# A graph network kernel on one core: first edge stage in another order, five source groups gathered later, another start, finer scatter turns

## The reference, cut to what matters

```python
# x: 100000 x 128, src and dst: 25000 edges, dst sorted (100000 * u**2)
def L0(x):      # edge messages, maximum by destination
    x_col = x[dst]
    feat = concatenate([x_col, x[src] - x_col], axis=-1)
    m = relu(feat @ W1 + b1) @ W2 + b2
    out = segment_max(m, dst, num_segments=x.shape[0])
    return where(isneginf(out), 0, out)
def L1(x):      # sum of neighbours, two-layer MLP, linear residual
    h = x + segment_sum(x[src], dst, num_segments=x.shape[0])
    h = maximum(h @ W1 + b1, 0) @ W2 + b2
    return x @ Wres + bres + h
x = layernorm(x + L0(x))
x = layernorm(x + L1(x))
```

## Time and profile before

| | us |
|---|---|
| median of 3 runs | 1114.47 |
| lowest and highest | 1114.39 and 1115.25 |
| the profiled execution, its own time | 1113.68 |
| its span (first to last instruction) | 1111.9 |
| PE busy in the span | 1068.9 (96%) |
| DVE busy | 934.9 (84%) |
| ACT busy | 896.9 (81%) |
| POOL busy | 765.8 (69%) |

### The profile page before, as it was taken

The page is one execution under the profiler, slowest core; times in us unless marked ns, Lnnn a source line. Parts: engine busy times, 40 slices in busy tenths (PEclk is TensorE's granted clock), DMA queues, the critical chain, the costliest instruction groups (busy, mean ns, idle before and its releaser), DMA issues.

```text
span 1111.9 us, 27074 instructions
## 1 busy us (share of the span) xinstructions
PE 1068.9 (96%) x7463; PEld 835.6 (75%) x7463; DVE 934.9 (84%) x3645; ACT 896.9 (81%) x3888; POOL 765.8 (69%) x798
## 2 busy tenths in 40 slices
PE   5899999999999999999899999999999999999995
PEld 3677877777666666666578888888888878888884
DVE  7799888897888888888868787878787789999993
ACT  2887878787888888888897888888888887777774
POOL 6777777777777777772047777777777777777712
PEclk9999999999999999999999999999999999999998
DMA  5788877875888888877576667676756566666652
GB/s 151 214 244 247 230 244 231 246 233 152 220 222 232 248 232 221 233 223 214 164 232 198 213 191 215 190 214 191 214 166 194 172 202 217 218 217 220 218 171 86
DMA packets 172255, 231.86 MB, mean 209 GB/s; under 512 B 25658, under 2 KB 90791, under 8 KB 172106
## 3 DMA queue, kind: packets, MB, share of 16 engines
q1 hardware_dynamic: 145434, 180.66, 52.0%
q0 software_dynamic: 25088, 48.94, 17.3%
q10 hardware_dynamic: 1584, 0.53, 0.2%
HBM read 129.48 MB, written 102.78 MB: 209 GB/s over the span
## 4 chain that ended last, share of the span: by engine, by line
PE 65%; POOL 19%; issue 8%; DVE 4%; ACT 2%; DMA 1%; SPq 0%; POOLq 0%; DVEq 0%; ACTq 0%
POOL edge_rows L522 17%; PE psY L1125 10%; PE psY L1126 10%; PE psH L1137 10%; PE psE L1118 6%; PE psT L1118 5%; PE psE L1257 4%; PE psE L1126 4%; PE psE L1125 4%; PE psE L1293 4%; PE psE L1248 3%; PE psE L1242 3%; PE psE L1240 3%; POOL xd_early L522 1%; DVE shared L758 1%
## 5 line engine op out<-in xcount | busy, mean ns | idle before, releaser
L1125 PE MATMUL psY<-wc,hT 128*128 128x128 f32 x1568 | 304.1, 276 | 0.5 <-DVE o_rows L646 0.4
L1126 PE MATMUL psY<-wcr,xT 128*128 128x128 f32 x1568 | 303.9, 276 | 0.0
L522 POOL DMA_INDIRECT edge_rows<-x1e_table,idx x196 | 188.8, 963 | 118.5 <-issue 59.4
L526 POOL DMA_INDIRECT out<-edge_rows,idx x196 | 195.0, 995 | 100.0 <-issue 61.9
L1125 PEld LDWEIGHTS psY<-wc,hT 128*128 128x128 f32 x1568 | 240.7, 192 | 13.3 <-issue 13.3
L949 ACT ACTIVATE junk<-psY 128x128 f32<-128x128 f32 x784 | 209.3, 302 | 49.3 <-PE psY L1126 49.1
L1126 PEld LDWEIGHTS psY<-wcr,xT 128*128 128x128 f32 x1568 | 238.8, 193 | 0.0
L522 POOL DMA_INDIRECT edge_rows<-in_x,idx x196 | 189.8, 968 | 65.5 <-issue 59.4
L609 DVE TENSOR_SCALAR x<-x_in,mv,rs 128x128 f32<-128x128 f32 x784 | 221.7, 361 | 0.6
L1137 PE MATMUL psH<-xT,wc 128*128 128x512 f32 x392 | 204.5, 604 | 6.2 <-ACT xT L944 5.5
L1118 PEld LDWEIGHTS psT<-ident,x 128*128 128x128 f32 x784 | 99.2, 143 | 110.1 <-issue 104.1
(11 more groups left out here) (125 smaller groups left out, 1993.4 us busy)
## 6 DMA issues: line engine op xcount, KB each, us to landing
x_in<-in_x SPq DMA_DIRECT2D x196, 256.0 KB
out<-o_rows SPq DMA_DIRECT2D x195, 256.0 KB
src_bc<-src_dram SPq DMA_DIRECT2D x49, 256.0 KB, 4.5
mask<-mask_dram SPq DMA_DIRECT2D x98, 128.0 KB
x1eT_spill<-x1eT SPq DMA_DIRECT2D x49, 256.0 KB, 2.4
x1e_table<-edge_rows SPq DMA_DIRECT2D x49, 256.0 KB, 3.5
x1e_table<-shared SPq DMA_DIRECT2D x49, 256.0 KB, 3.8
x1eT<-x1eT_spill SPq DMA_DIRECT2D x49, 256.0 KB, 3.1
```

The costliest lines, as they stand in the source:

```text
L522: nc.gpsimd.indirect_dma_start(to, None, table, bass.IndirectOffsetOnAxis(idx[:, what, t:t + 1], 0)).then_inc(landed[n % FLIGHT], 16)
L526: nc.gpsimd.indirect_dma_start(table, bass.IndirectOffsetOnAxis(idx[:, SCAT, t:t + 1], 0), frm, None, bounds_check=limit, oob_is_err=False ...
L1125: t_.matmul(to[:, cut(t)], h[:, cut(t)], wc2[:, :], start=t == 0, stop=False, skip_group_check=True)
L1126: last = t_.matmul(to[:, cut(t)], xt[:, cut(t)], wcr[:, :], start=False, stop=t == TILES - 1, skip_group_check=True)
```

## The change

Seven things change in the order and placing of work; no matrix product is added or removed.

1. In the first edge stage PE does `transpose_in(s+1)`, then `center_z(s-1)`, then `transpose_x1e(s-2)`, the reverse of before; `transpose_x1e` waits for one more `copy_xd`. DVE begins a step with the scan and the residual, and does the source statistics after `copy_xs`. ACT begins with `relu0`, and `copy_x1eT` comes behind the roots. The dense pieces of ACT and PE in `h` 0 and 1 change places.
2. The last five source groups (44 to 48) are gathered behind destination groups 12, 18, 24, 30 and 36, and no longer ahead of destination group 4.
3. SP loads unit 0 ahead of the source indices, and DVE takes its statistics first.
4. ACT issues the five bias loads after its first root, under a semaphore of their own. The copies of the combined weights go from DVE to ACT, and two of the weight products go behind the first dense product.
5. In the head ACT copies `xT` ahead of the root.
6. The first two `src_bc` loads are issued two steps' worth of queue entries earlier, at head step 6.
7. For groups 44 to 48, POOL waits for each slot's own count, worked out on DVE (`late_stores`, eight small instructions ahead of the second edge stage) and read with four register loads a turn.

```diff
-    SRC_FIRST = GROUPS
+    SRC_FIRST = GROUPS - 5
+    LATE_DST, LATE_EVERY = 12, 6
...
     def head(n):       # SP
...
+                if n == HEAD - 2:
+                    sp.wait_ge(s_srcst, 32)
+                    feed_s(0)
+                    feed_s(1)
...
+            load(0)
             sp.wait_ge(s_iz, 1)
             load_indices(0, src, s_is)
-            load(0)
             load(1)
...
             for g in range(SLOTS, GROUPS):
                 gather_dst(g)
+                if late_src_behind(g) is not None:
+                    gather_src(late_src_behind(g))
...
+            for g in range(LATE, WHOLE):
+                counts = late_needed(g - LATE)
+                pool.wait_ge(res_done, g + 1)
+                await_stores(counts)
+                for t in range(TILES):
+                    scatter_tile(g, t)
             for g in range(WHOLE, GROUPS):
                 pool.wait_ge(res_done, g + 1)
                 for t in range(TILES):
-                    await_stores(count if t < WHOLE_TILES else 16 * BODIES)
...
+                    await_stores(late_needed(SLOTS + t) if t < WHOLE_TILES else [16 * BODIES] * SLOTS)
+                    scatter_tile(g, t)
...
             def step_a(s, n, h):      # DVE
+                segment_max(s - 1)
+                residual0(s - 1)
                 both_recip(s)
                 scale_z(s)
-                segment_max(s - 1)
-                residual0(s - 1)
+                copy_xs(s + 1)
                 xs_stats(s)
                 xs_var(s)
-                copy_xs(s + 1)
...
             def head(n):       # ACT
-                if n == 0:
-                    copy_xT(0)
-                    root(0)
-                else:
-                    dense(n)
+                norm2_var(n - 3)
+                relu(n - 1)
+                copy_xT(n)
+                if n == 0:
+                    keep_weights()
+                root(n)
+                finish(n - 3)
...
             def step_a(s, n, h):      # ACT
+                relu0(s)
                 scale_xs(s)
-                relu0(s)
-                copy_x1eT(s - 2)
+                copy_xd(s + 1)
                 z_var(s - 1)
                 both_roots(s + 1)
-                copy_xd(s + 1)
+                copy_x1eT(s - 2)
...
             root(-2)
+            load_biases()
             root(-1)
-            act.wait_ge(s_w, 16 * 11)
+            act.wait_ge(s_b, 16 * 5)
...
             def step_a(s, n, h):      # PE
...
+                transpose_in(s + 1)
+                center_z(s - 1)
                 transpose_x1e(s - 2)
-                center_z(s - 1)
-                transpose_in(s + 1)
```

More of the change, by code:

```diff
@@ L159, in gnn_program @@
         s_w = sem("weights_loaded")
+        s_b = sem("biases_loaded")
         s_i = sem("indices_loaded")
@@ L254, in is_group, with late_src_behind @@
             return 0 <= g < GROUPS
+        def late_src_behind(g):
+            late, rest = divmod(g - LATE_DST, LATE_EVERY)
+            return SRC_FIRST + late if rest == 0 and 0 <= late < GROUPS - SRC_FIRST else None
         def src_number(g):
-            return TILES * (g + (SLOTS if g >= EARLY else 0))
+            if g < SRC_FIRST:
+                return TILES * (g + (SLOTS if g >= EARLY else 0))
+            late = g - SRC_FIRST
+            return TILES * (SRC_FIRST + LATE_DST + late * LATE_EVERY + 1 + late)
         def dst_number(g):
-            return TILES * (g + (EARLY if g < SLOTS else GROUPS))
+            if g < SLOTS:
+                return TILES * (EARLY + g)
+            return TILES * (SRC_FIRST + g + sum(late_src_behind(d) is not None for d in range(g)))
         def z_number(g):
@@ L554, in _, with stores_needed @@
                     gather(edge_rows[:, cut(g * TILES + t)], x1e_table, PLACE, g * TILES + t, z_number(g) + t)
[L556 to L561, removed]
+            def stores_needed(g):
+                top = g + SLOTS - 1
+                earlier = pool.value_load(stores_16[0:1, top:top + 1], min_val=0, max_val=16 * LAST)
+                return [pool.snap(earlier + 16)] * SLOTS
@@ L562, in await_stores, with late_needed, scatter_tile @@
+            def late_needed(at):
+                return [pool.value_load(late_16[0:1, at, k:k + 1], min_val=0, max_val=16 * BODIES) for k in range(SLOTS)]
+            def await_stores(counts):
                 for k in range(SLOTS):
-                    pool.wait_ge(stored[k], count)
+                    pool.wait_ge(stored[k], counts[k])
                 pool.nop().then_inc(s_turn, 1)
-            def last_group_of(g):
-                return g + SLOTS - 1 if g < LATE else g
+            def scatter_tile(g, t):
+                scatter(out, edge_rows[:, cut(g * TILES + t)], g * TILES + t, scatter_number(g) + t)
@@ L570, in _ @@
             pool.wait_ge(s_dv, SETUP_STEPS)
-            count = stores_needed(last_group_of(0))
-            for g in range(WHOLE):
+            counts = stores_needed(0)
+            for g in range(LATE):
                 pool.wait_ge(res_done, g + 1)
-                if g % SLOTS == 0 or g > LATE:
-                    await_stores(count)
+                if g % SLOTS == 0:
+                    await_stores(counts)
                 for t in range(TILES):
-                    if t == TILES - 1 and (g % SLOTS == SLOTS - 1 or g >= LATE):
-                        count = stores_needed(last_group_of(g + 1) if g + 1 < WHOLE else WHOLE)
-                    scatter(out, edge_rows[:, cut(g * TILES + t)], g * TILES + t, scatter_number(g) + t)
+                    if t == TILES - 1 and g % SLOTS == SLOTS - 1 and g + 1 < LATE:
+                        counts = stores_needed(g + 1)
+                    scatter_tile(g, t)
@@ L979, in dense @@
                 norm2_var(n - 3)
+                if n >= UNITS:
+                    root(n)
                 relu(n - 1)
-                root(n)
+                if n < UNITS:
+                    root(n)
                 copy_xT(n)
```

103 lines of the change are left out of this document (66 added, 37 removed).

## The result

| | before | changed |
|---|---|---|
| median of 6 runs, us | 1114.57 | 1128.78 |
| lowest and highest | 1113.79 to 1115.25 | 1127.79 to 1132.50 |
| span of the profiled execution | 1111.9 | 1127.2 |

The ratio is 1.0131, 95% interval 1.0117 to 1.0145: 1.3% slower, where I had forecast 8 us less and a range up to 1113. Rival D, the mask that comes late, is what happened, and stronger than I had priced it.

The account below looks back on a forecast made before the run. PE, nearly always busy, was taken as the bound, DVE and ACT close behind. Terms -3.4 - 0.5 - 0.6 - 1.2 + 0.3 - 2.6 = -8.0 gave 1105.7 against 1113.68, 1106.5 us for the median, range 1099 to 1113.

Parts of the forecast that it names:

- Rival D: First edge stage: SP issues the mask late, at T + 8.9 from step begin T; 1117.3 us at L 4.5; chance 0.20.
- What bounds the kernel: Whole kernel: PE nearly always busy; at most 13.2 us of idle time to gain in the first edge stage.
- L: Mask load in the first edge stage: time from issue to landing, thought near 3.8 us; at 4.4 the whole gain is gone.
- The start: Head and entry of matching: earlier unit 0 and src_bc loads cut waits, -3.4 us, bounds 1.0 to 4.8.
- The source groups: POOL's gathers: five groups moved later remove a 0.48 us wait for a destination tile, -0.5 us, between 0 and -0.7.
- The steady stage: First edge stage: four steps take 23.4 us against 23.52, residual wait traded for relu0; -0.6 us over 12 periods.
- The drain: End of the first edge stage: most of PE's 1.32 us wait for the last residual goes, -1.2 us, between 0 and -2.3.
- The clock in the drain: Last centring of the first edge stage: the clock would fall again after idling, keeping the term at -1.2, not -2.3.
- The late counts: Ahead of the second edge stage: eight small DVE instructions added, +0.3 us, between 0 and 8 x 0.49.
- the tail: Very end: one scatter instead of three behind the last store, -2.6 us, -1.3 if unit 194 lands late.

Follow-up runs that it names:

- e8: e1 with ACT's four squares of the dense unit spread, one tile each in h 0 and h 1, two in h 2: 1102.94 us, ratio to before 0.9898.
- e10: The kernel before with only source groups 44 to 48 gathered late, behind destination groups 12 to 36: 1112.55 us, ratio to before 0.9982.
- e5: e3 with the first two src_bc loads issued after the head again, as before the change: 1108.33 us, ratio to before 0.9944.
- e3: The changed kernel with the first edge stage's order on PE, ACT and DVE as before: 1105.61 us, ratio to before 0.9915.
- e1: The changed kernel with one line moved, SP issuing load_mask(s+1) ahead of the spill and not behind the three stores: 1106.81 us, ratio to before 0.9932.
- e4: e3 with all source groups gathered ahead of destination group 4 again: 1114.63 us, ratio to before 0.9994.
- e6: e3 with the scatter turns as before and without late_stores: 1108.49 us, ratio to before 0.9947.
- e9: e3 with ACT's four squares spread over the steps as in e8: 1105.33 us, ratio to before 0.9913.
- e2: The changed kernel with the mask issued right behind the spill, ahead of the two 256 KB stores: 1108.07 us, ratio to before 0.9937.
- e7: The changed kernel with each of the 128 partitions reading its 1 KB of mask from another place in memory: 1115.08 us, ratio to before 0.9999.

## Why the prediction was wrong, point by point

- **What bounds the kernel**: right. PE had 13 us of idle time in the stage, and the stage of e8, which has one more edit than the change, is 2.6 us shorter than before (278.03 against 280.63).
- **The mask (rival D)**: the step that failed is "I think L near 3.8", and behind it the chance of 0.08 for a clear loss. The mechanism, its place and its formula held; L measured 5.0 to the scan (4.9 to the landing), and the issue T + 9.2 and not 8.9. Both went the same way. A part of the 8.9 is a slip: the eight terms given for the end of the copy to `x1eT` add up to 7.5 and not 7.4. I took L from the store just ahead, because it is in the same queue, and not from the only other broadcast in the profile, 4.5 for `src_bc`, which the same group shows. A bound of 4.5 from twice the bytes looked like an upper end and was none. Even 4.5 gave 1117, counted from 5.76 a step; counted from the 5.86 that the same prediction has as its average it gives 5.98 - 5.86 = 0.12 a step and some 1112. So 4.5 already took most of the gain, and the real L was half a us beyond. A term with a threshold at 4.4 between rows of 3.8 and 4.5 deserved most of the chance, not a fifth. The fixed cost of about 2 us that the Trainium skill gives (DMA: Bandwidth & Descriptors, Anatomy of one DMA) would have put L lowest of all; that section is about transfers issued by GpSimd, and the mask is issued by SP. For this load in this traffic, 4.9 us, it was off by more than a factor of two.
- **The start**: -3.4 forecast, -4.1 measured against the trace of before and -3.0 against that of e10, which has the head of before; both are within its bounds. The mechanism was two causes, not one (e5).
- **The source groups**: -0.5 forecast. In the kernel before they are worth 2 by the medians, which no row puts down to them; in e3, behind the earlier start, 9. I had said that POOL could not follow then, but booked it as a condition, with no number, where it was the largest single term after the mask. The working was there: a lead of 3 to 4 us against a POOL that had none to spare.
- **The steady stage**: 23.4 us for four steps forecast, 23.44 measured with the mask put right. This term is right, the h 2 step on ACT included.
- **The drain**: -1.2 forecast. PE's waits there are 1.43 + 3.15 + 1.33 us in e1 against 0.62 + 1.67 + 1.32 + 0.74 in e3, +1.6, less 1.0 for a centring that in e1 ran at full clock: +0.6 by this sum. By the distance from the third last second product to the last transposes (`ident,shared`) it is 21.76 us in e1 against 21.84 before, so -0.1, and +0.9 without the luck of the clock. Either way not -1.2. What I had missed is what is late next: with the scan first, the reciprocal and the scaling stand between the residual and the centring, which waits for both. Chain of waits of e1:

```profile
541.99 1.29 DVE shared L787
...
543.98 0.21 DVE rs_e L767
...
544.21 0.70 DVE shared L777
...
545.04 0.92 PE psE L1324 x7
```

- **The clock in the drain**: in the old order the last centring stands behind waits of 1.67 and 1.32 us. With these same waits it took 2.08 us before and in e3, 2.07 in e4, 1.95 in e5, 1.76 in e6, 1.74 in e9 and 1.16 in e10. In the new order it stands behind one wait of 3.1 to 3.3 us, and took 2.04 us in the changed kernel, 1.72 in e2 and 1.13 in e1, e7 and e8. Rows of e10, e1 and the changed kernel:

```profile
553.57 1.16 PE L1270 MATMUL psE<-center,shared 128*128 128x128 f32 x8 [1.32 <-DVE shared L782]
```

```profile
550.62 1.13 PE L1324 MATMUL psE<-center,shared 128*128 128x128 f32 x8 [3.15 <-DVE shared L777]
```

```profile
572.02 2.04 PE L1324 MATMUL psE<-center,shared 128*128 128x128 f32 x8 [3.33 <-DVE shared L777]
```

  The granted clock of the 5 us around it was 1.00 in e10 and e1, and 0.66 in the changed kernel. The prediction took from the Trainium skill (TensorE: Matmul & The Clock Gate, What's actually happening) that the slow level is the default, to which the array returns when idle, and expected it here again. Eight traces agree, wholly or in part, and four (e1, e7, e8, e10) don't. So the waits by themselves do not decide it, and what does stays open. Up to 1 us of a kernel's time hangs on it.
- **The late counts**: +0.3 forecast, **the tail**: -2.6. The tail measured -3.1 (from 6.5 to 3.4 us behind the last rows), and e6, which undoes both, is 2.9 slower than e3 by the medians, 3.6 by the ratios: what the counts cost is too small for these runs to show.

Taken from the traces without the mask's wait (e1 against before), the start is -4.1, the stage with its gathers and drain -0.5 (up to the last transposes of the drain, 556.60 against 561.23), what follows +0.3 and the tail -3.1, in all -7.4. I had -3.4, -2.3, +0.3 and -2.6. The 1106.81 so close to my 1106.5 is luck in part: too little for the ends, too much for the stage, and a centring at full clock.

## What to carry to other kernels

When a copy is moved back on one engine, follow it into the queue whose order waits for it: what is issued behind that wait moves too, and a load with 7.4 us of room shows no wait until the room is gone. Write down the room (from the issue to the use) of everything behind a moved wait, both ends of it (here the issue moved 2.8 us back and the use 1.0 ahead), and take the latency of a broadcast load from another broadcast, never from a store. Where a term has a threshold inside its bounds, give the far side its full chance; and put the load that depends on nothing new ahead of the ones that do, which cost one line here and was worth 22 us.

A gain at the start is worth only as much as the next producer is ahead: POOL's gathers turned 4 us of lead into 5 us of waiting until five groups were taken out of their way (e4 against e3).

## What the runs showed of the hardware

- A broadcast load of 128 KB took 4.1 to 5.8 us from issue to use, 5.0 on average, with the DMA engines 77% busy, and 3.97 us once at 50%; 256 KB stores in the same queue took 2.2 to 4.1 by the medians of the runs. Moving the two stores behind the load took 0.6 us off it (4.9 to 4.3 from issue to landing; with the spill behind it as well it was 4.7), reading 128 different KB instead of one 1.2 (4.9 to 3.7).
- The same waits in the drain (1.67 and 1.32 us) left PE's next work at full clock in one kernel (1.16 us), slowed all of it in three others (2.07 and 2.08 us) and a part of it in three (1.74 to 1.95). A wait of 3.1 to 3.3 us in one piece did either too (1.13 and 2.04). In e4, with waits of 0.90, 1.61, 2.33 and 0.33 us between single transposes, the granted clock was 0.50 in 285 to 290 us.
